# Attention over edges: rows weighed two steps at a time, with a signal to TensorE for each two

## What is computed

```python
def _L1_gnn_ref(feat, src, dst, W, attn_l, attn_r):
    ft = (feat @ W).reshape(n, H, D)                    # H = 8, D = 32
    a1 = jnp.einsum('nhd,hd->nh', ft, attn_l)
    a2 = jnp.einsum('nhd,hd->nh', ft, attn_r)
    e = jax.nn.leaky_relu(a1[src] + a2[dst], negative_slope=ALPHA)
    m = jax.ops.segment_max(e, dst, num_segments=n)
    ex = jnp.exp(e - m[dst])
    s = jax.ops.segment_sum(ex, dst, num_segments=n)
    alpha = ex / s[dst]
    msg = ft[src] * alpha[:, :, None]
    out = jax.ops.segment_sum(msg, dst, num_segments=n)
    return jax.nn.elu(out.reshape(n, H * D))
```

## Time and profile before

| | us |
|---|---|
| median of 3 runs | 7891.57 |
| lowest, highest | 7881.64, 7893.34 |
| the profiled execution | 7877.83 |
| its span, first to last instruction | 7876.1 |
| attention: first to last weigh instruction | 4892.9 to 7369.2 |

### The profile page before, as it was taken

The page is one execution under the profiler, slowest core; times in us unless marked ns, Lnnn a source line. Parts: engine busy times, 40 slices in busy tenths (PEclk is TensorE's granted clock), DMA queues, the critical chain, the costliest instruction groups (busy, mean ns, idle before and its releaser), DMA issues. The chain is left out here.

```text
span 7876.1 us, 92000 instructions
## 1 busy us (share of the span) xinstructions
PE 4902.3 (62%) x20272; PEld 3673.7 (47%) x20272; DVE 3711.1 (47%) x10912; ACT 2475.0 (31%) x5104; POOL 5289.5 (67%) x5407
## 2 busy tenths in 40 slices
PE   4644444444443578777877775666666666666499
PEld 3533333333333455555556553444444444444266
DVE  6522222222222333333333334777777777777611
ACT  3533333333332122222222222333333333333111
POOL 0277777777776777777777774777777777777131
PEclk7555555555555577766677767777777777776699
DMA  4332222222222333333333333666666666666220
GB/s 151 85 80 78 83 79 81 81 78 81 81 78 76 82 82 81 86 88 83 81 82 85 89 82 85 187 191 192 193 189 187 190 199 188 188 191 187 79 91 20
DMA packets 588849, 903.65 MB, mean 115 GB/s; under 512 B 170033, under 2 KB 314905, under 8 KB 588055
## 3 DMA queue, kind: packets, MB, share of 16 engines
q0 software_dynamic: 204288, 353.98, 18.8%
q1 hardware_dynamic: 218582, 334.15, 13.6%
q10 hardware_dynamic: 165440, 209.63, 7.9%
HBM read 712.32 MB, written 210.89 MB: 117 GB/s over the span
## 5 line engine op out<-in xcount | busy, mean ns | idle before, releaser
L1653 POOL DMA_INDIRECT att_rows<-ft_rows,edges x1760 | 1832.4, 1041 | 736.6 <-issue 493.5
L744 POOL DMA_INDIRECT conv_rows<-table,sources x1760 | 1666.8, 947 | 599.7 <-issue 531.8
L744 POOL DMA_INDIRECT nod_rows<-table,sources x1760 | 1678.7, 954 | 552.1 <-issue 532.8
L978 PE MATMUL conv_pm<-conv_rows,conv_hot 128*128 128x64 f32 x3520 | 853.4, 424 | 1269.5 <-DVE conv_rows L914 1269.3
L1866 PE MATMUL att_pm<-att_rows,att_sel 128*128 128x264 f32 x3520 | 1383.7, 542 | 317.3 <-issue 230.5
L978 PEld LDWEIGHTS conv_pm<-conv_rows,conv_hot 128*128 128x128 f32 x3520 | 783.6, 328 | 1343.8 <-issue 1329.0
L1866 PEld LDWEIGHTS att_pm<-att_rows,att_sel 128*128 128x128 f32 x3520 | 859.2, 264 | 636.8 <-issue 297.8
L1147 PE MATMUL nod_pm<-nod_rows,nod_sel 128*128 128x32 f32 x3520 | 645.7, 339 | 508.6 <-DVE nod_rows L1396 507.0
L1147 PEld LDWEIGHTS nod_pm<-nod_rows,nod_sel 128*128 128x128 f32 x3520 | 628.4, 264 | 597.7 <-DVE nod_rows L1396 550.3
L832 ACT ACTIVATE conv_hot<-iota,edges 128x128 f32<-128x128 f32 x1760 | 537.3, 388 | 1104.3 <-PE conv_pm L978 1079.5
L2007 DVE TENSOR_TENSOR sums<-sums,att_pm 128x264 f32 x1760 | 747.4, 425 | 227.4 <-PE att_pm L1866 166.4
(11 more groups left out here) (386 smaller groups left out, 6573.8 us busy)
## 6 DMA issues: line engine op xcount, KB each, us to landing
selections<-conv_hot ACTq DMA_DIRECT2D x220, 512.0 KB
nod_sel<-selections SPq DMA_DIRECT2D x440, 256.0 KB
att_sel<-selections SPq DMA_DIRECT2D x440, 256.0 KB
att_bc<-places SPq DMA_DIRECT2D x110, 512.0 KB
conv_rows<-table,sources POOLq DMA_INDIRECT x1760, 2.4
nod_rows<-table,sources POOLq DMA_INDIRECT x1760, 2.4
att_rows<-ft_rows,edges POOLq DMA_INDIRECT x1760
ft_rows<-nod_ft ACTq DMA_DIRECT2D x25, 544.0 KB
```

Source lines behind the costliest of these rows:

```text
L744: pool.indirect_dma_start(out=rows[:, k % SLOTS, :], out_offset=None, in_=table, in_offset=bass.IndirectOffsetOnAxis(ap=K.srct[:, k:k + 1] ...
L978: ins = nc.tensor.matmul(pm[i % RING][:, k, :], hot[:, q * QUAD // SECT % PARTS, (q * QUAD + k) % SECT, :], rows[:, (q * QUAD + k) % SLOTS ...
L1653: pool.indirect_dma_start(out=rows[:, k % SLOTS, :], out_offset=None, in_=K.ftd, in_offset=bass.IndirectOffsetOnAxis(ap=sources[:, k:k + 1 ...
```

## The change

A group of four steps is weighed by two instructions of two steps each (128 x 528 numbers), and each signals `weighed`. TensorE waits for `weighed` at every second step instead of once a group, for the instruction that weighed these two steps. ScalarE's threshold before it overwrites the weights is doubled, since the count runs twice as fast.

```diff
                 if n >= 2:
-                    act.wait_ge(weighed, (n - 1) * NQ)
+                    act.wait_ge(weighed, (n - 1) * NQ * 2)
...
                 if k0 == 0:
-                    pe.wait_ge(weighed, b * NQ + q + 1)
                     pe.wait_ge(sel_loaded[q], b * 16 + 16)
                 for k in range(k0, k1):
                     s = q * QUAD + k
+                    if k % 2 == 0:
+                        pe.wait_ge(weighed, (b * SEGS + s) // 2 + 1)
                     pe.wait_ge(added, b * SEGS + s + 1)
...
-                s0 = slot(i, q * QUAD)
-                r = rows[:, s0:s0 + QUAD, 0:WIDTH].rearrange("p s (h d) -> p s h d", d=H1)
-                p = pw[:, b % 2, q * QUAD * HEADS:(q + 1) * QUAD * HEADS].rearrange("p (s h) -> p s h", h=HEADS)
-                tt(r, r, p.unsqueeze(3).to_broadcast([P, QUAD, HEADS, H1]), ALU.mult).then_inc(weighed, 1)
+                for at in range(q * QUAD, (q + 1) * QUAD, 2):
+                    s0 = slot(i, at)
+                    r = rows[:, s0:s0 + 2, 0:WIDTH].rearrange("p s (h d) -> p s h d", d=H1)
+                    p = pw[:, b % 2, at * HEADS:(at + 2) * HEADS].rearrange("p (s h) -> p s h", h=HEADS)
+                    tt(r, r, p.unsqueeze(3).to_broadcast([P, 2, HEADS, H1]), ALU.mult).then_inc(weighed, 1)
```

## The result

| | us |
|---|---|
| before, median of 8 runs | 7889.58 (7881.64 to 7893.34) |
| after, median of 8 runs | 7912.26 (7904.89 to 7914.79) |
| ratio, 95% interval | 1.0029 [1.0021, 1.0038] |

The changed kernel is 0.29% slower, some 23 us. The span of its profiled execution is 7902.8 us against 7876.1, and the stretch from the first weigh instruction to the last is 4898.5 to 7398.2 where it was 4892.9 to 7369.2. That is 2499.7 us against 2476.3, start to start, so 23.4 us of the difference arise in the attention stage (0.6 of them because the last one is now a second half). The stage also began 5.6 us later.

What follows compares the result with a forecast made beforehand. The prediction took VectorE, by its own work and register work, to set the attention stage's time. The split's 30.8 us less 1.8 and 6 given back made +23, so 7891.6 + 23 = 7915 us, range 7892 to 7940.

Steps and rivals of the forecast that it cites:

- The bound: Attention stage: VectorE's own work and register work set the time; GpSimd close behind, its only slack 149.5 us of 2300.
- TensorE's finer wait gives nothing: TensorE's matmuls: each wait on `added` ends after the one on `weighed`, so waiting for two steps gains 0.
- the other end: TensorE's 440 added semaphore waits: 18 us if each delayed VectorE by 40 ns; 0 was taken.
- The price of the split: VectorE's weigh: fixed cost of 0.07 us added 440 times, 30.8 us; with 0.06 to 0.08, 26 to 35.
- The bound of 0.167 from single durations: VectorE's weigh: two halves last 167 ns more than one whole by durations of single instructions, giving 73 us.
- What is given back: VectorE's waits take in part of the split's cost: 1.8 us before ScalarE's exponentials, 6 us before turned rows.
- The term of 6 us: VectorE's waits for turned rows: a later VectorE waits less; between 0 and 14.9 us can come back, 6 taken.
- The lower end of its range: The forecast's own lowest added time: +9 us, from 26.4 - 1.8 - 14.9; its upper end was +35.
- The seam: GpSimd's gathers get in between the halves: 0.58 of the waiting left, at most 70 us of GpSimd's time saved.
- The gathers set the pace: Rival: the cycle follows GpSimd's occupation, so 70 us come back and VectorE's 31 hide: 7822. Chance 0.08.
- The cost is covered: Rival: VectorE's waits for exponentials and turned rows, 40 us, take in 25 or more of the 31: 7898. Chance 0.10.
- Full price: Rival: the second half waits for the first to finish, +73 - 2, giving 7963. Chance 0.12.

Runs made afterwards that it cites:

- the two doses of work on GpSimd: Kernel before with small memsets added on GpSimd: 440, ahead of every fourth gather, 7888.82 us (1.0005); 1760, ahead of every gather, 8011.42 us (1.0164).
- the moved weigh: Kernel before with each weigh instruction moved behind the two additions that followed it: 7896.48 us (1.0018); the changed kernel with the same move: 7828.52 us (0.9928).
- the pieces moved: Changed kernel with the weighs moved and the pieces that finish a group of windows put ahead of the weigh: 7798.38 us (0.9896).
- the split alone: Kernel before with two weigh instructions of two steps each, only the second signalling, TensorE waiting once a group: 7905.12 us (1.0029).
- the waits alone: Kernel before with TensorE waiting for weighed rows at every second step, rows still weighed four steps at a time: 7879.24 us (0.9996).
- the held half: Kernel before with the weigh split into two halves, the second waiting for the first on a semaphore: 7954.75 us (1.0095).

## Why the prediction was right, point by point

- **The bound.** VectorE with its register work set the pace, and GpSimd had a small slack. Shown by the two doses of work on GpSimd (1.0005, then 1.0164), by the scan that follows the moved weigh without idle time, by the 0.3 us left ahead of `whole` with the pieces moved, and by the products of TensorE, which lay ready before the additions that idled. One thing was only half read: VectorE's lead over GpSimd is so small that after a change of order alone late gathers hold VectorE in most blocks.
- **TensorE's finer wait gives nothing.** Shown by the split alone. The prediction said that TensorE's added semaphore waits have no row in the trace before; they have one, at line 1865, 440 instructions of 51 ns, so the other end should have been 440 x 0.051 = 22 us and not 18. The value taken, 0, is what the waits alone gave (0.9996, interval 0.9987 to 1.0005). That no matmul would be put down to the weigh in the changed profile was wrong by the letter: 49.2 us are, by coincidence as shown above.
- **The price of the split.** 0.07 us was forecast and 0.070 measured, start to start. The bound of 0.167 from single durations did not apply, since nothing holds the second half. With a wait between the halves the interval grows by 0.116 to 0.735 and the time to 1.0095.
- **What is given back.** 30.8 - 1.8 - 6 = 23 was forecast and 23.4 measured in the stage, but the middle is put together differently. Between the starts of all VectorE's instructions of the stage, the intervals of the weigh pairs and behind them grew by 31.9 us. Those ahead of the instruction that takes ScalarE's exponentials (2024) shrank by 1.8, as forecast; those ahead of the scan of the turned rows by 2.0, not 6; those between sums by 2.0, those ahead of `along` by 1.4, and 1.3 are spread. The term of 6 us was too large by 4, and small ones I had not listed made up for it. That the sum comes within 1 us is luck; that it is some 23 and not 31 or 73 is not. (The lower end of its range, 26.4 - 1.8 - 14.9, is 9.7 and not 9, which changes nothing.)
- **The seam.** That a gather gets in between the halves is right; 0.58 of the held time was estimated to be left. Counted over the gathers that begin under a weigh, the time above the usual 947 ns fell from 126 to 78 us, 0.62 of it. All gathers together gained 36 us (1041 to 1021 ns) where 70 was the upper bound, which took all lengthened gathers for the weigh's. That it is the weigh and not any work of VectorE that holds a gather shows in the kernel before: where VectorE had last started an addition, which reads one input from PSUM, 305 gathers began and none took over 1.00 us; where it had last started a weigh, 269 of 376 did.
- **The rivals.** "The gathers set the pace" was the serious one. It was rightly put at a low chance for this order of work; its condition holds with the moved weigh, where the halves gain 68 us. "The cost is covered" failed: the two waits it counted on took in 1.8 + 2.0 = 3.8 us and not 25. "Full price" is what the held half paid.

## What to carry to other kernels

Splitting an elementwise instruction costs its engine one fixed price a piece, here 0.070 us where no piece waits for another, and shortens what the instruction holds up elsewhere; whether that is a loss or a gain is settled by which engine waits for which, and the same split was worth +23 us and -68 us in two orders of the same work. An idle time in front of an instruction that has the same length every time is likely the engine's own register work, whatever releaser is named for it. A finer signal is worth nothing if another wait on the same instruction always ends later.

## What was not expected of the hardware

A move that leaves every instruction as it was lengthened the mean gather from 1041 to 1095 ns, and VectorE lost in waiting, most of it for turned rows, all that the move had saved it. GpSimd's own issue gap partly covers small work: 406 memsets of 0.197 us (80 us) shortened its "issue" idle time by 40 us, from 455.8 to 415.3.
